# A decoder layer on one core: decay, query-key and value products restricted to the lower triangle

## The chip, the core and the metric

The kernel runs on one core of one Trainium2 chip. The core has TensorE (matmuls, results in eight banks of 512 f32 columns in PSUM), VectorE (DVE), ScalarE (ACT), GpSimd (POOL) and SyncE (SP), which only issues DMAs. Each engine works through its own queue in order; semaphores tie them together. The metric is the device time of one execution in microseconds (us), the median of several runs.

## What is computed

One decoder layer on 128 sequences of 128 tokens and 256 features: self-attention with one head, then a cross stage with eight heads of 32 features, gated and causal (queries and keys have the same length), then an FFN with a low-rank adapter. The change touches the cross stage alone. Its reference, cut:

```python
mask = jnp.tril(jnp.ones((seq, seq), dtype=bool))
F_act = jnp.where(mask, Fmat, -jnp.inf)          # Fmat[i, j] = csum[i] - csum[j]
Dtilde = F_act + itilde[..., None, :]
D = jnp.exp(Dtilde - max_d)
Ctilde = jnp.einsum('bhid,bhjd->bhij', qh, kh) * D / TAU
maxit = jnp.maximum(jnp.abs(jnp.sum(Ctilde, axis=-1, keepdims=True)), jnp.exp(-max_d))
Htilde = jnp.einsum('bhij,bhjd->bhid', Ctilde, vh) / (maxit + 1e-06)
```

D is zero wherever key j comes after query i, so of the 128x128 products per sequence and head only the lower triangle counts.

## The kernel before

The 128 sequences are taken in 32 groups of four (G = 4, a sequence of the group is called a batch b). The work is a software pipeline: in step `it` group it+1 is normalised (coming), group it is in self-attention (own), group it-1 is in the cross stage (cross) and group it-2 in the FFN (ffn). Steps 2 to 30 are one loop body, the rest is unrolled; steps 2 to 31 hold own, cross and ffn together. The order on every engine is the order in which its part of `step` is written out by hand; semaphores with a count per step (`c_ok`, `dexp_ok`, `pv_mm` and so on) connect the engines.

The cross stage on TensorE, for keys on the partitions and queries on the columns:

- `qk(t)` (L1255), t = 0 and 1, two batches each: for each batch 8 f32 matmuls, one per head. Head 4f+r has its 32 features on partitions 32r to 32r+31 of `ctxT` (stationary, 32x128) and `xn2T` (moving, 128 columns), so the four r work on four row tiles of the array and write four banks (QKB = TA, QQ, GT, DD). It stands among the eight FFN blocks `up(i)` (L1231, L1244), which use the full array. `keep_qk` (L653) on ScalarE copies the banks into `QKs`, four copies of 512 columns per call.
- `decay(b, hf)` (L1323): the logarithm of D for four heads, 512 columns, in DD or QQ: one bf16 matmul of `parts` with `moving`, and one that adds `later`, a mask of -1e30 above the diagonal. Eight such chunks per step. `dexp` (L674) on ScalarE takes the exponential into `dx` (the memory of `qT`), `weigh_qk` (L963) on VectorE multiplies it with `QKs` into `C`.
- `pv(b)` (L1338): 8 f32 matmuls, one per head, stationary the 32 value columns of `vc` (128x32), moving the 128 columns of `C`; head h writes partitions 32(h%4) on. Then `hs`, `turn_h`, `ht` and `head_sums` normalise.

The calls of L1387 to L1451 interleave these with `down` (L1302), `low_rank`, `adapt` (L1320), `turn_probs`, `mix` (L1375), `values` (L1382) of the other groups. `pv(b)` waits for the last chunk of C of its batch; `decay` waits until the chunk before last has been read by ScalarE.

`vc` is made by GpSimd (L555) early in the step; SyncE (L457 to L482) waits for it before it loads the next `ctxn`, then waits for `parts`.

## Time and profile before

| | us |
|---|---|
| median of 3 runs (1965.82 to 1968.34) | 1966.54 |
| the profiled execution | 1969.64 |
| its span, first to last instruction | 1967.8 |
| TensorE busy | 1905.0 (97%) |
| VectorE busy | 1509.3 (77%) |
| ScalarE busy | 1092.4 (56%) |
| GpSimd busy | 316.1 (16%) |

The profile splits TensorE into PE (matmuls) and PEld (loads of the stationary operand), which overlap. "L1269" is a line of the kernel. A row of a group gives the line, the engine, the operation, output<-inputs and the shapes; a row of the timeline begins with the start and the length in us, and merges neighbours of the same kind (x16), so that the last one's start is the first start plus the length less one's own duration. An f32 matmul appears as two records.

### The profile page before, as it was taken

The numbers are of one execution on the slowest core, as the hardware profiler recorded it, in microseconds if no ns is written. First come the engines' busy times: TensorE is split into PE (matmuls) and PEld (weight loads), VectorE is DVE, ScalarE is ACT, GpSimd is POOL, SyncE is SP. The second block draws the span as 40 slices with busy tenths as digits, with TensorE's granted clock in tenths as the row PEclk, the third lists the DMA queues.
The fourth block names the chain that finished last, engine by engine and source line by source line (L and its number), as shares of the span: only waits on it lengthen the run. The fifth ranks groups of instructions, "written<-read, shape, count | busy, mean of one in ns | idle before, by whom it ended". The sixth has DMA issues, their size and how long they took to land.

```text
span 1967.8 us, 44983 instructions
## 1 busy us (share of the span) xinstructions
PE 1905.0 (97%) x14612; PEld 1397.4 (71%) x14612; DVE 1509.3 (77%) x4352; ACT 1092.4 (56%) x2440; POOL 316.1 (16%) x259
## 2 busy tenths in 40 slices
PE   4689999999999999999999999999999999999988
PEld 3457777777777777777777777777777777777766
DVE  6588877778787778787778878777878777887742
ACT  2355556655556655556655555665555665555551
POOL 1111011111111111101111101111110111110110
PEclk9699999999999999999999999999999999999999
DMA  4101111111111111111111111111111111111100
GB/s 116 33 24 36 31 33 44 44 33 44 22 33 44 44 41 36 26 40 33 44 44 33 43 23 33 44 44 36 41 22 33 44 44 44 33 35 31 24 13 23
DMA packets 200751, 73.21 MB, mean 37 GB/s; under 512 B 148353, under 2 KB 200194, under 8 KB 200722
## 3 DMA queue, kind: packets, MB, share of 16 engines
q1 hardware_dynamic: 200722, 72.84, 14.5%
q8 instruction: 16, 0.26, 0.1%
q14 instruction: 13, 0.11, 0.0%
HBM read 53.93 MB, written 16.78 MB: 36 GB/s over the span
## 4 chain that ended last, share of the span: by engine, by line
PE 94%; DVE 4%; ACT 1%; issue 0%; DMA 0%; SPq 0%; DVEq 0%; ACTq 0%
PE UA L1302 16%; PE UB L1302 5%; PE UB L1244 5%; PE UA L1244 5%; PE TB L1244 5%; PE PV L1244 5%; PE UA L1252 3%; PE TA L1269 3%; PE TB L1382 3%; PE GT L1312 3%; PE TA L1382 3%; PE TA L1209 3%; PE TA L1113 3%; PE TB L1113 3%; PE UA L1320 2%; PE QQ L1332 2%
## 5 line engine op out<-in xcount | busy, mean ns | idle before, releaser
L1302 PE MATMUL UA<-W2f,hs_all 128*128 128x256 f32 x1536 | 349.0, 380 | 3.8 <-DVE ot L952 3.1
L1302 PEld LDWEIGHTS UA<-W2f,hs_all 128*128 128x128 f32 x1536 | 286.5, 190 | 63.1 <-issue 13.9
L968 DVE TENSOR_TENSOR C<-qT,QKs 128x512 f32<-128x512 f32 x256 | 166.6, 690 | 175.6 <-ACT qT L677 167.9
L562 POOL TENSOR_TENSOR Ng<-HT,gnw_b 128x256 f32<-128x256 f32 x128 | 96.1, 751 | 885.2 <-ACT HT L690 885.2
L543 POOL TENSOR_TENSOR xg<-x,gnb_b 128x1024 f32<-128x1024 f32 x32 | 76.4, 2386 | 679.5 <-ACT ot L632 646.0
L1302 PE MATMUL UB<-W2f,hs_all 128*128 128x256 f32 x512 | 115.8, 379 | 0.0
L576 ACT ACTIVATE lv<-ve 128x4 f32<-128x4 f32 x95 | 19.0, 200 | 161.2 <-DVE ve L795 161.2
L1302 PEld LDWEIGHTS UB<-W2f,hs_all 128*128 128x128 f32 x512 | 95.0, 190 | 11.7
L658 ACT ACTIVATE QKs<-TA 128x512 f32<-128x512 f32 x64 | 38.3, 599 | 105.6 <-PE DD L1269 105.6
L668 ACT ACTIVATE hs_all<-UA,b1c 128x512 f32<-128x512 f32 x64 | 44.0, 687 | 80.4 <-PE TB L1252 80.4
L1269 PEld LDWEIGHTS TA<-xn2T,ctxT 32*128 32x128 f32 x512 | 63.2, 190 | 26.2 <-issue 23.7
L549 POOL TENSOR_TENSOR x<-xin,cvp 128x1024 f32<-128x1024 f32 x32 | 76.4, 2387 | 26.7 <-DVE c L841 14.0
L902 DVE TENSOR_TENSOR_SCAN csum<-ones,lsig 128x128 f32<-128x128 f32 x32 | 79.6, 2489 | 1.1
L677 ACT ACTIVATE qT<-QQ 128x512 f32<-128x512 f32 x128 | 75.7, 591 | 6.3 <-PE QQ L1334 0.5
L1269 PE MATMUL TA<-xn2T,ctxT 32*128 32x128 f32 x512 | 75.6, 287 | 2.9 <-ACT QKs L658 2.2
L677 ACT ACTIVATE qT<-DD 128x512 f32<-128x512 f32 x128 | 75.1, 586 | 3.0 <-PE DD L1334 3.0
L1269 PE MATMUL QQ<-xn2T,ctxT 32*128 32x128 f32 x512 | 75.6, 288 | 0.0
L1269 PE MATMUL GT<-xn2T,ctxT 32*128 32x128 f32 x512 | 75.6, 288 | 0.0
L1269 PE MATMUL DD<-xn2T,ctxT 32*128 32x128 f32 x512 | 75.6, 288 | 0.0
L1252 PE MATMUL UA<-T,E 32*128 32x512 f32 x128 | 71.7, 640 | 0.0
L1252 PE MATMUL TB<-T,E 32*128 32x512 f32 x128 | 71.7, 640 | 0.0
L1252 PE MATMUL PV<-T,E 32*128 32x512 f32 x128 | 71.7, 640 | 0.0
(310 smaller groups left out, 5378.6 us busy)
## 6 DMA issues: line engine op xcount, KB each, us to landing
xin<-x SPq DMA_DIRECT2D x32, 512.0 KB, 3.5
ctxn<-ctx SPq DMA_DIRECT2D x32, 512.0 KB, 3.8
bands<-ctx SPq DMA_DIRECT2D x256, 64.0 KB, 2.0
out<-ot SPq DMA_DIRECT2D x32, 512.0 KB, 3.0
Ev<-xn SPq DMA_DIRECT2D x512, 1.0 KB
hs_all<-L_ffn_W SPq DMA_DIRECT2D x4, 512.0 KB, 8.9
T<-tok SPq DMA_DIRECT2D x128, 2.0 KB
moving<-parts SPq DMA_DIRECT2D x96, 8.0 KB, 1.8
```

The source lines that it names most:

```text
L543: pool.tensor_tensor(xg[:, :, :], x2[:, :, :], gnb_b[:, :].unsqueeze(1).broadcast_to([P, G, D]), ALU.add).then_inc(xg_ok.h, 1)
L549: pool.tensor_tensor(x2[:, :, :], xin[:, :, :], cvp[:, :].unsqueeze(1).broadcast_to([P, G, D]), ALU.add).then_inc(xb_ok.h, 1)
L562: pool.tensor_tensor(Ng[:, b, :].rearrange("p (k n) -> p k n", k=2), HT[:, b % 2, :, 0:P], gnw_b[:, :].rearrange("p (k n) -> p k n", k=2), ...
L677: act.activation(dx[hf], DB[hf][:, :], ACT.Exp)\
L902: dve.tensor_tensor_scan(csum[:, :], ones[:, :], lsig[:, :], 0.0, ALU.mult, ALU.add)\
L968: dve.tensor_tensor(C[:, b % 2, 4 * hf:4 * hf + 4, :].rearrange("p h i -> p (h i)"), dx[hf], QKs[:, b, 4 * hf:4 * hf + 4, :].rearrange("p ...
L1113: ins = pe.matmul(TAB[m][:, :], A_w[:, k, m * P:(m + 1) * P], xn1T[:, k, :], start=(k == 0), stop=(k == 1))
L1244: pe.matmul(UP[i % 4][:, :], w[:, k, hc * P:(hc + 1) * P], xt[:, k, :], start=(w is W1h and xt is xn3h and k == 0), stop=False)
L1252: pe.matmul(UP[r][:, :], E[32 * r:32 * r + 32, j, :], T[32 * r:32 * r + 32, :], start=False, stop=True).then_inc(up_mm.h, 1)
L1269: ins = pe.matmul(QKB[r][:, (2 * b + f) * P:(2 * b + f + 1) * P], ctxT[lane, f, tok], xn2T[lane, f, tok], start=True, stop=True)
L1302: ins = pe.matmul(OB[b][:, 0:D], hs_all[:, k, b * S:(b + 1) * S], W2f[:, k, :], start=(i == 0), stop=(i == KH - 1))
L1382: ins = pe.matmul(TAB[b // 2][:, (b % 2) * D:(b % 2) * D + D], pxT[:, k, b * S:(b + 1) * S], Wvp[:, k, :], start=(k == 0), stop=(k == 1))
```

## The change

With H = 64, the queries of a batch are split into late ones (64 to 127), which need all 128 keys, and early ones (0 to 63), which need only keys 0 to 63. The quarter early query, late key is no longer computed.

- Query-key: for each batch 8 matmuls with the same 128-column stationaries and the 64 late columns, then 8 with stationaries of 64 columns (the early keys) and the 64 early columns. Heads 0 to 3 (f = 0) go to partitions 0 to 63, heads 4 to 7 to partitions 64 to 127, so that two head groups share one block of 64 columns. A bank now holds 384 columns instead of 512.
- Decay: six chunks per step instead of eight. Three belong to a pair of batches: chunk 0 and chunk 2 are the late columns of the first and the second batch, 8 heads by 64; chunk 1 holds the early columns of both, packed on the upper and lower partitions by two matmuls of 64 stationary columns. `dexp` and `weigh_qk` run six times.
- Value product: for each batch 8 matmuls of 64 late columns from `vc`, and 8 of 64 early columns from `vcs`. `vcs` holds the early keys' values of heads 0 to 3 on partitions 0 to 63 and of heads 4 to 7 on partitions 64 to 127; its other halves stay zero. Two DMAs per step fill it from `vc`.
- `keep_qk` copies 384 columns. Two setup buffers move from `QKs` to `C`, setup gets one copy more (the mask for the lower partitions) and one memset (`vcs`).

The diff, cut to its core:

```diff
+H = S // 2
+CHUNKS = 3 * G // 2
...
-        QKs = sb("QKs", [P, G, HEADS, P])
+        QKs = sb("QKs", [P, G, 3 * CB, H])
+        vcs = sb("vcs", [P, G, 2, P])
...
-        C = sb("C", [P, 2, HEADS, P])
+        C = sb("C", [P, 4, HEADS, H])
...
+        vcs_loaded = per_step("vcs_loaded", CROSS, 2 * 16)
...
+                if CROSS.on(it):
+                    sp.wait_ge(vc_ok.h, vc_ok.at(it, 1))
+                    for f in range(2):
+                        sp.dma_start(vcs[H * f:H * f + H, :, f, :], vc[0:H, :, P * f:P * f + P])\
+                          .then_inc(vcs_loaded.h, 16)
...
-                        act.activation(QKs[:, 2 * t:2 * t + 2, r::4, :],
-                                       QKB[r][:, :].rearrange("p (b f i) -> p b f i", b=2, f=2), ACT.Copy)\
+                        act.activation(QKs[:, 2 * t:2 * t + 2, r::CB, :],
+                                       QKB[r][:, 0:6 * H].rearrange("p (b f i) -> p b f i", b=2, f=3), ACT.Copy)\
...
-                def dexp(b, hf):
-                    act.wait_ge(d_mm.h, d_mm.at(it, 2 * b + hf + 1))
-                    act.wait_ge(c_ok.h, c_ok.at(it, max(2 * b + hf - 1, 0)))
-                    act.activation(dx[hf], DB[hf][:, :], ACT.Exp)\
+                def dexp(k):
+                    act.wait_ge(d_mm.h, d_mm.at(it, k + 1))
+                    act.wait_ge(c_ok.h, c_ok.at(it, max(k - 1, 0)))
+                    act.activation(dx[k % 2], DB[k % 2][:, :], ACT.Exp)\
...
+            done(dve.tensor_copy(later[H:P, 0:H], later[0:H, 0:H]))
...
-                def weigh_qk(b, hf):
-                    k = 2 * b + hf
+                def weigh_qk(k):
+                    t, j = k // 3, k % 3
                     dve.wait_ge(dexp_ok.h, dexp_ok.at(it, k + 1))
-                    dve.wait_ge(QKs_ok.h, QKs_ok.at(it, 4 * (b // 2) + 4))
+                    dve.wait_ge(QKs_ok.h, QKs_ok.at(it, 4 * t + 4))
+                    if j == 1:
+                        dve.tensor_tensor(C[:, 2 + t, :, :].rearrange("p (b r) i -> p b (r i)", b=2),
+                                          dx[k % 2].rearrange("p (b x) -> p b x", b=2),
+                                          QKs[:, 2 * t:2 * t + 2, HEADS:HEADS + CB, :].rearrange("p b r i -> p b (r i)"),
+                                          ALU.mult).then_inc(c_ok.h, 1)
+                        return
+                    b = 2 * t + j // 2
                     dve.wait_ge(pv_mm.h, pv_mm.at(it, max(b - 1, 0)))
-                    dve.tensor_tensor(C[:, b % 2, 4 * hf:4 * hf + 4, :].rearrange("p h i -> p (h i)"), dx[hf],
-                                      QKs[:, b, 4 * hf:4 * hf + 4, :].rearrange("p h i -> p (h i)"), ALU.mult)\
+                    dve.tensor_tensor(C[:, b % 2, :, :].rearrange("p h i -> p (h i)"), dx[k % 2],
+                                      QKs[:, b, 0:HEADS, :].rearrange("p h i -> p (h i)"), ALU.mult)\
                         .then_inc(c_ok.h, 1)
...
+                        early, late = slice(tok.start, tok.start + H), slice(tok.start + H, tok.stop)
                         for f in range(2):
                             for r in range(4):
                                 lane = slice(32 * r, 32 * r + 32)
-                                ins = pe.matmul(QKB[r][:, (2 * b + f) * P:(2 * b + f + 1) * P],
-                                                ctxT[lane, f, tok], xn2T[lane, f, tok], start=True, stop=True)
+                                pe.matmul(QKB[r][:, (3 * b + f) * H:(3 * b + f + 1) * H],
+                                          ctxT[lane, f, tok], xn2T[lane, f, late], start=True, stop=True)
+                        for f in range(2):
+                            for r in range(4):
+                                lane = slice(32 * r, 32 * r + 32)
+                                ins = pe.matmul(QKB[r][H * f:H * f + H, (3 * b + 2) * H:(3 * b + 3) * H],
+                                                ctxT[lane, f, early], xn2T[lane, f, early], start=True, stop=True)
...
-                def decay(b, hf):
-
-                    k = 2 * b + hf
+                def decay(k):
+
+                    t, j = k // 3, k % 3
                     pe.wait_ge(dexp_ok.h, dexp_ok.at(it, max(k - 1, 0)))
                     if k == 0:
                         pe.wait_ge(QKs_ok.h, QKs_ok.at(it, 8))
                         pe.wait_ge(parts_ok.h, parts_ok.at(it, 1))
                         pe.wait_ge(moving_loaded.h, moving_loaded.at(it, 3 * 16))
-                    h0 = HEADS * b + 4 * hf
-                    pe.matmul(DB[hf][:, :], parts[:, 0, :], moving[:, h0:h0 + 4, :],
-                              start=True, stop=True)
-                    ins = pe.matmul(DB[hf][:, :], ident_h[:, :], later[:, :].unsqueeze(1).broadcast_to([P, 4, P]),
+                    bank = DB[k % 2]
+                    if j == 1:
+                        heads = moving[:, 2 * t * HEADS:(2 * t + 2) * HEADS, 0:H].rearrange(
+                            "p (b f r) i -> p f b r i", b=2, f=2)
+                        for f in range(2):
+                            pe.matmul(bank[H * f:H * f + H, :], parts[:, 0, 0:H], heads[:, f, :, :, :],
+                                      start=True, stop=True)
+                    else:
+                        b = 2 * t + j // 2
+                        pe.matmul(bank[:, :], parts[:, 0, :], moving[:, HEADS * b:HEADS * b + HEADS, H:P],
+                                  start=True, stop=True)
+                    mask = later[:, 0:H] if j == 1 else later[:, H:P]
+                    ins = pe.matmul(bank[:, :], ident_h[:, :], mask.unsqueeze(1).broadcast_to([P, HEADS, H]),
                                     start=False, stop=True, skip_group_check=True)
...
-                    pe.wait_ge(c_ok.h, c_ok.at(it, 2 * b + 2))
+                    pe.wait_ge(c_ok.h, c_ok.at(it, 3 * (b // 2) + 2 + b % 2))
                     if b == 0:
                         pe.wait_ge(vc_ok.h, vc_ok.at(it, 1))
+                        pe.wait_ge(vcs_loaded.h, vcs_loaded.at(it, 2 * 16))
                     elif b == 1:
                         pe.wait_ge(h_ok.h, h_ok.at(it, 6))
                     bank = PB[b % 2]
                     for h in range(HEADS):
                         q = 32 * (h % 4)
-                        ins = pe.matmul(bank[q:q + 32, (h // 4) * P:(h // 4 + 1) * P], vc[:, b, HD * h:HD * h + HD],
-                                        C[:, b % 2, h, :], start=True, stop=True)
+                        pe.matmul(bank[q:q + 32, (h // 4) * P + H:(h // 4 + 1) * P], vc[:, b, HD * h:HD * h + HD],
+                                  C[:, b % 2, h, :], start=True, stop=True)
+                    for f in range(2):
+                        for r in range(4):
+                            ins = pe.matmul(bank[HD * r:HD * r + HD, f * P:f * P + H], vcs[:, b, f, HD * r:HD * r + HD],
+                                            C[:, 2 + b // 2, 4 * (b % 2) + r, :], start=True, stop=True)
...
-                    decay(0, 0)
-                    decay(0, 1)
+                    decay(0)
+                    decay(1)
                 if ffn:
                     down(0)
                     low_rank()
                 if cross:
-                    decay(1, 0)
+                    decay(2)
                     pv(0)
-                    decay(1, 1)
+                    decay(3)
                     turn_em()
                 if own:
                     turn_probs()
                 if cross:
                     turn_h(0)
-                    decay(2, 0)
                 if ffn:
                     adapt(0)
                 if cross:
                     pv(1)
-                    decay(2, 1)
+                    decay(4)
                 if own:
                     mix(0)
                 if cross:
@@ -1412,9 +1445,8 @@
                 if own:
                     mix(1)
                 if cross:
-                    decay(3, 0)
                     pv(2)
-                    decay(3, 1)
+                    decay(5)
```

What stands on TensorE for one query-key call, before: the end of `up(4)`, then four groups like the one shown (the shape is stationary columns x moving columns), then `up(5)`.

```order
L1244 MATMUL UA<-xn3l,W1h 128x512 x2
L1257 REGISTER_ALU
L1269 MATMUL TA<-xn2T,ctxT 128x128
L1269 MATMUL QQ<-xn2T,ctxT 128x128
L1269 MATMUL GT<-xn2T,ctxT 128x128
L1269 MATMUL DD<-xn2T,ctxT 128x128
...
L1239 REGISTER_ALU
L1244 MATMUL UB<-xn3h,W1h 128x512 x2
```

And after, where the two kinds take turns batch by batch:

```order
L1258 MATMUL UA<-xn3l,W1h 128x512 x2
L1271 REGISTER_ALU
L1284 MATMUL TA<-xn2T,ctxT 128x64
L1284 MATMUL QQ<-xn2T,ctxT 128x64
L1284 MATMUL GT<-xn2T,ctxT 128x64
L1284 MATMUL DD<-xn2T,ctxT 128x64
...
L1289 MATMUL TA<-xn2T,ctxT 64x64
L1289 MATMUL QQ<-xn2T,ctxT 64x64
L1289 MATMUL GT<-xn2T,ctxT 64x64
L1289 MATMUL DD<-xn2T,ctxT 64x64
...
L1258 MATMUL UB<-xn3h,W1h 128x512 x2
```

Each of the four banks now gets 8 matmuls per call where it got 4, in four blocks of two shapes.

Around the value product of batch 1, on TensorE, before:

```order
L1356 MATMUL PV<-centre,HS 128x132 x2
L1326 REGISTER_ALU
L1332 MATMUL DD<-moving,parts 128x512
L1334 MATMUL DD<-later,ident_h 128x512
L1319 ISA
L1320 MATMUL UA<-Ev,gT 128x256
L1349 MATMUL UB<-C,vc 32x128 x8
L1332 MATMUL QQ<-moving,parts 128x512
L1334 MATMUL QQ<-later,ident_h 128x512
```

And after:

```order
L1390 MATMUL PV<-centre,HS 128x132 x2
L1339 ISA
L1340 MATMUL UA<-Ev,gT 128x256
L1370 REGISTER_ALU
L1379 MATMUL UB<-C,vc 32x64 x8
L1383 MATMUL UB<-C,vcs 32x64 x8
L1356 MATMUL DD<-moving,parts 64x512 x2
L1363 MATMUL DD<-later,ident_h 128x512
L1409 MATMUL TA<-PT,xn 128x128 x4
```

The chunk between `turn_h(0)` and `adapt(0)` is gone, the value product has two halves, and the chunk behind it is an early one (chunk 4).

## Rows read from the trace of the kernel before

**Rows 1.** The page: busy time by engine, and the chain that ended last.

```profile
PE 1905.0 (97%) x14612; PEld 1397.4 (71%) x14612; DVE 1509.3 (77%) x4352; ACT 1092.4 (56%) x2440; POOL 316.1 (16%) x259
...
PE 94%; DVE 4%; ACT 1%; issue 0%; DMA 0%; SPq 0%; DVEq 0%; ACTq 0%
```

**Rows 2.** Busy time in two full steps, by window; columns as in the header.

```profile
core 0: us, PE busy (x) PEld busy (x) DVE busy (x) ACT busy (x) POOL busy (x), PEclk, DMA share, GB/s
998.60:1056.90 58.30, 58.30 (x453) 42.82 (x452) 46.66 (x136) 33.92 (x77) 9.70 (x7) 1.00 0.15 37
1056.90:1115.20 58.30, 58.30 (x453) 42.83 (x452) 46.64 (x136) 33.92 (x77) 9.70 (x7) 1.00 0.15 37
```

**Rows 3.** Timeline of PE around one query-key call: start us, length us, instruction.

```profile
1011.85 0.63 PE L1244 MATMUL UA<-xn3l,W1h 128*128 128x512 f32 x2
1012.40 0.37 PE L1269 MATMUL TA<-xn2T,ctxT 32*128 32x128 f32 x1
...
1012.42 0.37 PE L1269 MATMUL DD<-xn2T,ctxT 32*128 32x128 f32 x1
1012.62 0.27 PE L1269 MATMUL TA<-xn2T,ctxT 32*128 32x128 f32 x1
...
1012.73 0.27 PE L1269 MATMUL TA<-xn2T,ctxT 32*128 32x128 f32 x1
...
1013.31 0.27 PE L1269 MATMUL DD<-xn2T,ctxT 32*128 32x128 f32 x1
1013.51 0.50 PE L1244 MATMUL UB<-xn3h,W1h 128*128 128x512 f32 x1
```

**Rows 4.** Timeline of setup: products with one moving column.

```profile
24.66 0.53 PEld L1151 LDWEIGHTS QQ<-bcol,QKs 128*128 128x128 f32 x4
24.68 0.58 PE L1151 MATMUL QQ<-bcol,QKs 128*128 128x1 f32 x4
```

**Rows 5.** Timeline of PE around two value products and two decay chunks.

```profile
1026.84 0.38 PE L1334 MATMUL DD<-later,ident_h 128*128 128x512 bf16 x1
...
1027.15 0.38 PEld L1349 LDWEIGHTS PV<-C,vc 128*32 128x32 f32 x16 [0.43 <-issue]
1027.15 0.65 PE L1349 MATMUL PV<-C,vc 128*32 128x128 f32 x16
...
1027.73 0.39 PE L1332 MATMUL QQ<-moving,parts 99*128 99x512 bf16 x1
...
1029.17 0.38 PE L1332 MATMUL DD<-moving,parts 99*128 99x512 bf16 x1
...
1029.39 0.38 PE L1334 MATMUL DD<-later,ident_h 128*128 128x512 bf16 x1
...
1029.61 0.59 PE L1320 MATMUL UA<-Ev,gT 128*128 128x256 f32 x2
...
1031.16 1.05 PE L1375 MATMUL TA<-PT,xn 128*128 128x128 f32 x8
...
1033.39 0.38 PE L1332 MATMUL DD<-moving,parts 99*128 99x512 bf16 x1
```

**Rows 6.** Timeline of setup: pairs of 64-column tiles.

```profile
37.06 1.16 PE L1168 MATMUL GT<-ident,hs_all 128*64 128x128 f32 x16
```

**Rows 7.** Groups by line and form: count, then busy us and mean ns.

```profile
L677 ACT ACTIVATE qT<-QQ 128x512 f32<-128x512 f32 x128 | 75.7, 591 | 6.3 <-PE QQ L1334 0.5
L658 ACT ACTIVATE QKs<-TA 128x512 f32<-128x512 f32 x64 | 38.3, 599 | 105.6 <-PE DD L1269 105.6
L683 ACT ACTIVATE HS<-UB 128x256 f32<-128x256 f32 x64 | 24.7, 385 | 20.3 <-PE UB L1349 20.1
L968 DVE TENSOR_TENSOR C<-qT,QKs 128x512 f32<-128x512 f32 x256 | 166.6, 690 | 175.6 <-ACT qT L677 167.9
```

**Rows 8.** Timelines of POOL and of SP's queue early in the same step.

```profile
1008.91 1.96 POOL L555 TENSOR_TENSOR vc<-ctxn 128x992 f32<-128x992 f32 x1
...
1011.04 0.38 SPq L465 DMA_DIRECT2D ctxn<-ctx  x1
1014.57 0.56 SPq L469 DMA_DIRECT2D moving<-parts  x1
```

**Rows 9.** The cross step without an FFN, by window; columns as in rows 2.

```profile
79.00:99.00 20.00, 12.54 (x113) 7.94 (x117) 13.68 (x42) 11.17 (x33) 0.10 (x1) 0.53 0.27 54
```

More of the change, by code:

```diff
@@ L284, in build @@
         wT = stage[:, 1536:3072].rearrange("p (w k d) -> p w k d", w=3, k=KD)
-        wp = stage[:, 3072:3584].rearrange("p (k o) -> p k o", k=KD)
-        bB = stage[:, 3584:4096].rearrange("p (w k n) -> p w k n", w=2, k=KD)
+        spare = C[:, :, :, :].rearrange("p a b c -> p (a b c)")
+        wp = spare[:, 0:512].rearrange("p (k o) -> p k o", k=KD)
+        bB = spare[:, 512:1024].rearrange("p (w k n) -> p w k n", w=2, k=KD)
         bcol = sb("bcol", [P, 6])
@@ L328, in build @@
         em_mm = per_step("em_mm", CROSS, 1)
-        d_mm = per_step("d_mm", CROSS, 2 * G)
+        d_mm = per_step("d_mm", CROSS, CHUNKS)
         qk_mm = per_step("qk_mm", CROSS, 2)
@@ L350, in build @@
         em_ok = per_step("em_ok", CROSS, 1)
[L351 removed]
+        dexp_ok = per_step("dexp_ok", CROSS, CHUNKS)
         HS_ok = per_step("HS_ok", CROSS, G)
@@ L373, in build @@
         zo_ok = per_step("zo_ok", FFN, 1)
-        c_ok = per_step("c_ok", CROSS, 2 * G)
+        c_ok = per_step("c_ok", CROSS, CHUNKS)
         x2_ok = per_step("x2_ok", SELF, G)
@@ L530, in _ @@
                                pattern=[[-8, G], [-32, CB], [-1, R]], channel_multiplier=1)
-            for t in (WgT, Z, Zo, E, T, Ev, em):
+            for t in (WgT, Z, Zo, E, T, Ev, em, vcs):
                 pool.memset(t[tuple([slice(None)] * len(t.shape))], 0.0)
@@ L714, in step @@
                         .then_inc(em_ok.h, 1)
-                    dexp(0, 0)
-                    dexp(0, 1)
+                    dexp(0)
+                    dexp(1)
                 if coming:
@@ L721, in step @@
                 if cross:
-                    dexp(1, 0)
+                    dexp(2)
                     hs(0)
-                    dexp(1, 1)
+                    dexp(3)
                     ht(0)
@@ L728, in step @@
                 if cross:
-                    dexp(2, 0)
                     hs(1)
-                    dexp(2, 1)
+                    dexp(4)
                 if own:
@@ L744, in step @@
                 if cross:
-                    dexp(3, 0)
                     hs(2)
-                    dexp(3, 1)
+                    dexp(5)
                     ht(2)
@@ L1001, in step @@
                 if cross:
-                    weigh_qk(0, 0)
-                    weigh_qk(0, 1)
+                    weigh_qk(0)
+                    weigh_qk(1)
                 if ffn:
@@ L1009, in step @@
                 if cross:
-                    weigh_qk(1, 0)
-                    weigh_qk(1, 1)
+                    weigh_qk(2)
+                    weigh_qk(3)
                     dve.wait_ge(em_mm.h, em_mm.at(it, 1))
@@ L1014, in step @@
                     head_sums(0)
-                    weigh_qk(2, 0)
-                    weigh_qk(2, 1)
+                    weigh_qk(4)
                 if ffn:
@@ L1028, in step @@
                 if cross:
-                    weigh_qk(3, 0)
-                    weigh_qk(3, 1)
+                    weigh_qk(5)
                 if coming:
@@ L1459 @@
 V_BIAS = V_WT + 2 + 2 + 2 + 4
-SETUP_V = V_BIAS + 2 + 1 + 2 + 1 + 8 + 1
+SETUP_V = V_BIAS + 2 + 1 + 1 + 2 + 1 + 8 + 1
 def kernel(**inputs):
```

3 lines of the change are left out of this document (1 added, 2 removed).

## The prediction, made before the changed kernel was run

> **What bounds the kernel now.** I read the page first: TensorE is busy 97% of the span and carries 94% of the chain that ended last [rows 1]. Then two neighbouring steps of the loop, by window: each takes 58.30 us, TensorE is busy for all of it at the full granted clock, VectorE for 46.7 and ScalarE for 33.9 [rows 2]. There are 30 such full steps (the four batches of a group in their cross stage while another group is in its self stage and a third in its FFN), 1,749 of 1,967.8 us; the rest is setup, one cross step without an FFN at the start, and the drain at the end. So a full step costs what TensorE's stream costs, and everything the change saves on the other two engines is hidden. The question is how TensorE's stream changes, and the timeline of its instructions gives the prices. The profiled execution took 1969.64 us, span 1967.8; I make the sum as a difference and put it on the median of the three runs, 1966.54, from which the profile is 3.1 us off.
>
> **How a small product is priced.** An f32 product is two records for each of its matmuls. In the query-key call four 32-row tiles run side by side: the four first records start within 0.02 us, and then a new group of four starts every 0.11 us (1012.62, 1012.73, ... 1013.29) [rows 3]. 0.11 us is what 128 moving columns cost, but it is also what the stationary operand costs: in setup, four records of a product with 1 moving column and the same 128 stationary columns take 0.58 us, 0.25 of it the last one's own latency, so 0.11 each [rows 4]. Halving the moving columns of a product whose stationary is still 128 columns wide therefore saves nothing. The second price is that of a change of the array's shape. Between two full-array matmuls of 512 bf16 columns the starts are 0.22 apart; from the last full one to the first 32-column one it is 0.31 (1026.84 to 1027.15), and back from the last 32-column record (its start is 1027.15 + 0.65 - 0.27 = 1027.53) to the full array 0.20 where 0.11 would be its own width [rows 5]. The query-key call shows the same: 1012.08 (1011.85 + 0.63 - 0.40) to 1012.40 is 0.32 against a pitch of 0.23, and 1013.31 to 1013.51 is 0.20 [rows 3]. Each change costs about 0.09 us, and behind it the first load is not covered: 0.10 for 128 f32 columns (the second group starts 0.22 after the first, not 0.11), so by width 0.05 for 64 and 0.03 for 32.
>
> **Query-key (L1263 to L1271), per call, two calls per step.** Before: 8 groups, 1.10 us from 1012.40 to 1013.51 [rows 3]. After: per batch 4 groups with 128-column stationaries and 64 moving columns, then 8 matmuls on 32x64 tiles, and so twice. The late part keeps its 4 groups of 0.11 per batch; only the last of each ends 0.05 earlier: -0.11. The early part is new: if the upper and the lower column tiles run together it is 2 groups of 0.06 (64 columns, twice) per batch: +0.22. Three more changes of shape (late to early, back, late to early) at 0.09: +0.28; the uncovered first loads behind them, 0.05 + 0.10 + 0.05: +0.21; and 0.02 of staggered starts for each of three more bursts: +0.06. Sum +0.67 per call, **+1.33 per step**. Bounds: no row shows a change from a 32x128 to a 32x64 tile. If it is free, only the early groups are added, +0.22 per call, +0.44 per step; if the two column tiles take turns, +0.22 more per call, +1.8 per step. I take the middle, since every change of shape in rows 3 and 5 costs 0.09, and since 64-column tiles do run in pairs in setup: 16 records in 1.16 us, 0.06 apart, where 128 f32 columns one after the other would need 0.11 each [rows 6].
> The Trainium skill (TensorEngine Tiling (Array Packing), Key Properties) says that changing the tiling mode drains TensorE, while tiles of one mode work independently, and lists 32x128 and 32x64 as different configurations. By that rule the term is +1.33; if only the rows of the array counted it would be +0.44. The trace agrees on the changes that it has (0.09 us each).
>
> **Decay (L1323 to L1336), per step.** Before: 8 chunks of two matmuls at 0.22 [rows 5], 3.52. After: four late chunks as before, and two early ones: two 64-column matmuls side by side (0.22), the mask (0.22), and changes of shape. The first early chunk stands between full-array work: two changes and one uncovered load, 0.24, so 0.68. The second comes right behind pv(1), where a change is due anyway: 0.58. Sum 1.76 + 1.26 = 3.02: **-0.50 per step**. Bounds: -0.88 if the changes are free, -0.07 if the two 64-column matmuls take turns; again rows 6 are nearest to side by side.
>
> **Value product (L1338 to L1351), per batch, four per step.** Before: 16 records in groups of four, 0.58 us from 1027.15 to 1027.73 [rows 5]. After: 32 records of 64 columns, all on 128x32 tiles, so no change of shape in between: 8 groups of 0.055 to 0.06 in the place of 4 of 0.11, the same columns. The 16 loads of 32 columns take 0.38 from first start to last end at 0.11 latency each [rows 5], so they overlap and hide behind 0.055. **+0.03 per batch, +0.1 per step**; bounds 0 and, if a group cannot start sooner than 0.11 after the last, +0.38 per batch, +1.5 per step.
>
> **What is hidden.** ScalarE loses two exponentials (0.59 each) and a fifth of eight copies of 512 columns (0.60 against 0.39 at 256, so about 0.49 at 384); VectorE loses two products of 0.65 to 0.69 [rows 7]. None of it is on the path of a full step. Cover: there is now no decay between mix(1) and pv(2). pv(2) needs chunk 4, whose mask ends about 0.4 us after its start, then 0.59 of ScalarE, 0.69 of VectorE and some 0.2 of handing over; TensorE has mix(0), turn_h(1) and mix(1) in between, 1031.16 to 1033.39 [rows 5], 2.2 us, so some 0.5 remains. If it failed, pv(2) would wait that long. The same holds for chunk 5 and pv(3). The two DMAs that fill vcs stand on SyncE's queue behind vc (ready at 1010.87) and ahead of the ctxn load; each issue is 0.4 to 0.6 us, and the queue is idle from 1011.42 to 1014.57 [rows 8]; pv(0) wants them at 1027, so nothing. Setup gets one more small copy and a memset, ahead of work that waits elsewhere: nothing.
>
> **The two partial steps.** In the cross step without an FFN the granted clock is 0.53 [rows 9], the lower of two levels (1.2 GHz), so TensorE's extra work costs double there, about 2 us; against it stand waits on ScalarE and VectorE that shrink by about as much. At the end the same waits shrink by 1 or 2 us. I count nothing, -3 to +2.
>
> **Sum.** 1.33 - 0.50 + 0.10 = +0.93 per step, times 30 = +28 us: 1966.5 + 28 = **1994 us**. The change cuts columns only where the stationary operand and the shape of the array do not matter, in a quarter of the decay.
>
> **Rivals.**
> (a) Free changes of shape, faster than before. Place: the three new boundaries in each query-key call and those around the early decay chunks. If these cost nothing and the value product costs nothing, the step changes by 0.44 - 0.88 = -0.44, -13 us, 1953. It decides as soon as all three new boundaries and loads of a call cost less than 0.2 us together instead of 0.55. For it: no row shows such a boundary between two shapes with the same 32 rows. Against: all other boundaries show 0.09. 12%.
> (b) No change to be measured: either the loads of four 32-row tiles are quicker than the 0.11 of rows 4 (the late groups then shrink to 0.06, -0.45 per call, and the step's sum is +0.03), or the query-key boundaries alone are free (+0.44 - 0.50 + 0.10 = +0.04). About 1968. 12%.
> (c) The early tiles take turns, or handing over costs a bit more at 64 columns: +0.45 per step, 1994 + 13 = 2007. 11%.
> (d) Starts are the limit. A change that doubles the records pays if a record cannot follow the last in less than 0.027 us (16 records in 0.37 us of starts is 0.025 on average in rows 5, and rows 3 give 0.028). Then the value product costs +1.5 and the early query-key groups +1.3 more per step, 2.8 x 30 = 84 us: 2075. Against it: within a group the starts are under 0.01 apart. 8%.
> The Trainium skill (TensorE: Matmul & The Clock Gate, "Wait — 56ns, not 53.3ns?") states that start-to-start never falls below about 25 ns however small a matmul is; taken for every tile it would give rival (d), but its section on packing small matmuls gives 4 ns between tiles, and the starts in rows 3 are that close.
>
> **How the numbers follow.** Forecast as summed, 1980 to 2005 by the small uncertainties of its terms: 57%. Taking (a) to (d): slower 57 + 11 + 8 = 76%, same 12%, faster 12%. The range leaves out (d) and most of (a): 1960 to 2030. About 0.2%, 4 us, is what a measurement of this kernel can tell from no change.
>
> **What would show it.** In the profile after, a full step of about 59.2 us with TensorE still busy throughout. A query-key call of 1.75 to 1.8 us to the next FFN matmul, with groups of the late part 0.11 apart, of the early part 0.06, and gaps of about 0.15 at the three boundaries. A value product of 0.6 us with 32 records; early decay chunks of 0.6 to 0.7. ScalarE and VectorE at 32 and 45 us per step. The prediction is wrong if late groups start 0.06 apart, if there is no gap between late and early, if the value product takes 0.9, or if TensorE begins to wait for C ahead of pv(2) or pv(3).

## The result, and the profile after

The changed kernel takes 1993.39 us in the median of four runs (1990.73 to 1998.63), the kernel before 1967.05 in the same comparison (four runs, 1965.82 to 1968.34): ratio 1.0137, 95% interval 1.0115 to 1.0159, so 26 us slower. The prediction was 1994 us.

The page of the changed kernel, busy time by engine, and one line of its costliest groups (the ScalarE copy of the scores):

```profile
PE 1934.3 (97%) x18644; PEld 1437.5 (72%) x18644; DVE 1469.1 (74%) x4289; ACT 1042.5 (52%) x2376; POOL 318.0 (16%) x260
...
L668 ACT ACTIVATE QKs<-TA 128x384 f32<-128x384 f32 x64 | 31.6, 493 | 165.3 <-PE DD L1289 165.3
```

Against [rows 1] TensorE is busy 29 us more, VectorE 40 and ScalarE 50 us less. What was saved, was saved on the other engines; the chain that ended last is TensorE's for 94%, as before. A full step by window (columns as in rows 2; the next step reads the same):

```profile
1013.92:1073.09 59.17, 59.17 (x579) 44.01 (x578) 45.44 (x134) 32.37 (x75) 9.73 (x7) 1.00 0.16 41
```

A full step is 59.17 us for 58.30 [rows 2], and TensorE is still busy for all of it. 0.87 x 30 = 26.1 us, of the 26.3 by which the medians differ; in the medians the partial steps add nothing. (The profiled execution, at 1998.63, is 5 us over its median. There is one trace of this kernel, which does not show what part of it took longer than usual; the run without the value DMAs below has the same step and took 1992.65, and 4.3 us of the 6.0 between the two stand ahead of the second full step.) The step repeats to 0.02 us from one to the next, so in what follows the length of a full step is the measure, and the time of a run is given beside it.

**The query-key call.** Timeline of TensorE around the first half of a call in the changed kernel. L1284 is the late product, L1289 the early one; of each group of four simultaneous tiles one record stands here:

```profile
1027.73 0.32 PE L1284 MATMUL TA<-xn2T,ctxT 32*128 32x64 f32 x1
...
1027.89 0.27 PE L1284 MATMUL TA<-xn2T,ctxT 32*128 32x64 f32 x1
...
1028.00 0.27 PE L1284 MATMUL TA<-xn2T,ctxT 32*128 32x64 f32 x1
...
1028.13 0.27 PE L1284 MATMUL DD<-xn2T,ctxT 32*128 32x64 f32 x1
1028.33 0.27 PE L1289 MATMUL TA<-xn2T,ctxT 32*64 32x64 f32 x1
...
1028.48 0.22 PE L1289 MATMUL DD<-xn2T,ctxT 32*64 32x64 f32 x1
1028.63 0.32 PE L1284 MATMUL TA<-xn2T,ctxT 32*128 32x64 f32 x1
...
1029.39 0.22 PE L1289 MATMUL DD<-xn2T,ctxT 32*64 32x64 f32 x1
1029.53 0.74 PE L1258 MATMUL UB<-xn3h,W1h 128*128 128x512 f32 x2
```

The late groups start 0.11 apart with 64 columns as they did with 128 [rows 3]. From the last late record to the first early one it is 0.20 (1028.13 to 1028.33); the sixteen early records start within 0.15; from the last of them to the next late one, or to the FFN's product, 0.15 (1028.48 to 1028.63, 1029.39 to 1029.53). One batch takes 0.90 us, the call 1.80 (1027.73 to 1029.53) where it was 1.10: +0.70 per call, +1.40 per step.

**Values and decay.** Timeline of TensorE around the first early chunk, and from the value product of batch 0 to the early chunk ahead of the mixing products (L1363 mask, L1379 late and L1383 early values, L1360 late and L1356 early decay):

```profile
1037.25 0.38 PE L1363 MATMUL DD<-later,ident_h 128*128 128x512 bf16 x1
1037.56 0.41 PE L1356 MATMUL QQ<-moving,parts 99*64 99x512 bf16 x2
...
1038.12 3.62 PE L1322 MATMUL UA<-W2f,hs_all 128*128 128x256 f32 x16
...
1044.07 0.43 PE L1379 MATMUL PV<-C,vc 128*32 128x64 f32 x16
1044.31 0.41 PE L1383 MATMUL PV<-C,vcs 128*32 128x64 f32 x16
1044.65 0.39 PE L1360 MATMUL QQ<-moving,parts 99*128 99x512 bf16 x1
1044.88 0.38 PE L1363 MATMUL QQ<-later,ident_h 128*128 128x512 bf16 x1
1045.10 0.27 PE L1398 MATMUL GT<-ident,em 128*128 128x128 f32 x1
1045.21 0.60 PE L1403 MATMUL TB<-ident,y 128*128 128x128 f32 x4
1045.64 0.62 PE L1390 MATMUL PV<-centre,HS 128*128 128x132 f32 x4
1046.10 0.59 PE L1340 MATMUL UA<-Ev,gT 128*128 128x256 f32 x2
1046.62 0.43 PE L1379 MATMUL UB<-C,vc 128*32 128x64 f32 x16
...
1047.20 0.41 PE L1356 MATMUL DD<-moving,parts 99*64 99x512 bf16 x2
1047.54 0.39 PE L1363 MATMUL DD<-later,ident_h 128*128 128x512 bf16 x1
```

A value product is 0.58 us (1044.07 to 1044.65), as before, with twice the records. An early chunk behind a value product is 0.34 for the pair of 64-column matmuls (1047.20 to 1047.54) and 0.23 for the mask, 0.57; a late chunk is 0.45 (1044.65 to 1045.10). The first early chunk stands between full-array work: from the mask of the late chunk before it to the FFN product behind it 0.87 us pass (1037.25 to 1038.12), 0.22 of them that mask's own, so 0.65 to 0.66.

### The profile page after: what moved, and what is told of

The parts are those of the page before. It is cut to its first block, busy times and chain, and to the rows that moved or that the text cites. A ratio compares the mean times of both kernels' runs of the same rounds, so it can differ in the third digit from the quotient of the medians.

```text
span 1996.6 us, 52832 instructions
## 1 busy us (share of the span) xinstructions
PE 1934.3 (97%) x18644; PEld 1437.5 (72%) x18644; DVE 1469.1 (74%) x4289; ACT 1042.5 (52%) x2376; POOL 318.0 (16%) x260
## 4 chain that ended last, share of the span: by engine, by line
PE 94%; DVE 4%; ACT 1%; issue 0%; DMA 0%; SPq 0%; DVEq 0%; ACTq 0%
PE UA L1322 16%; PE UB L1322 5%; PE UB L1258 5%; PE UA L1258 5%; PE TB L1258 5%; PE PV L1258 5%; PE TA L1284 3%; PE UA L1266 3%; PE TB L1416 3%; PE GT L1332 3%; PE TA L1416 3%; PE TA L1223 3%; PE TA L1127 3%; PE TB L1127 3%; PE UA L1340 2%; PE QQ L1115 2%
## 5 line engine op out<-in xcount | busy, mean ns | idle before, releaser
L984 DVE TENSOR_TENSOR C<-qT,QKs 128x512 f32<-128x512 f32 x128 | 88.6, 692 | 219.4 <-ACT qT L687 206.3
L668 ACT ACTIVATE QKs<-TA 128x384 f32<-128x384 f32 x64 | 31.6, 493 | 165.3 <-PE DD L1289 165.3
L1284 PEld LDWEIGHTS TA<-xn2T,ctxT 32*128 32x128 f32 x512 | 67.7, 189 | 30.3 <-issue 23.9
L1284 PE MATMUL TA<-xn2T,ctxT 32*128 32x64 f32 x512 | 85.4, 287 | 2.5 <-ACT QKs L668 1.8
L1284 PE MATMUL QQ<-xn2T,ctxT 32*128 32x64 f32 x512 | 85.5, 287 | 0.0
L1284 PE MATMUL GT<-xn2T,ctxT 32*128 32x64 f32 x512 | 85.5, 287 | 0.0
L1284 PE MATMUL DD<-xn2T,ctxT 32*128 32x64 f32 x512 | 85.5, 287 | 0.0
L1266 PE MATMUL UB<-T,E 32*128 32x512 f32 x128 | 71.7, 640 | 0.0
L1416 PE MATMUL TA<-Wvp,pxT 128*128 128x256 f32 x256 | 67.3, 387 | 0.7 <-ACT pxT L714 0.7
```

Source lines behind the costliest of these rows:

```text
L984: dve.tensor_tensor(C[:, b % 2, :, :].rearrange("p h i -> p (h i)"), dx[k % 2], QKs[:, b, 0:HEADS, :].rearrange("p h i -> p (h i)"), ALU.m ...
L1266: pe.matmul(UP[r][:, :], E[32 * r:32 * r + 32, j, :], T[32 * r:32 * r + 32, :], start=False, stop=True).then_inc(up_mm.h, 1)
L1284: pe.matmul(QKB[r][:, (3 * b + f) * H:(3 * b + f + 1) * H], ctxT[lane, f, tok], xn2T[lane, f, late], start=True, stop=True)
L1416: ins = pe.matmul(TAB[b // 2][:, (b % 2) * D:(b % 2) * D + D], pxT[:, k, b * S:(b + 1) * S], Wvp[:, k, :], start=(k == 0), stop=(k == 1))
```

## The experiments

The theory: the step is TensorE's own stream, and in it the stationary operand and the changes of the array's shape cost, not the moving columns. Rivals: the number of products and loads costs (then order doesn't matter); the columns do cost (then halving them helped); the engines that were relieved, or the new DMAs, play a part.

### One change of shape in a call instead of three (late_first)

```diff
-for b in range(2): late(b); early(b)
+for b in range(2): late(b)
+for b in range(2): early(b)
```

> Of the changed kernel, each query-key call runs the late products of both batches first and then the early products of both, so that a call changes the matmul's shape once inside instead of three times; nothing is left out. If the price of the early products is the change of shape (the trace of the changed kernel shows 0.20 us before the first early product and 0.15 us before the next late one), two of these stretches go, and a call falls from 1.806 to about 1.49 us, a full step by 0.63 us and the kernel by 19 us, to about 1974 us. If the price is the number of products and of weight loads, the call stays at 1.8 us and the kernel at 1993 us.

Measured: 1976.28 us (six runs) against 1968.29 for the kernel before, ratio 1.0039, interval 1.0027 to 1.0052. The step, and the timeline of a call at its start, at the boundary and at its end:

```profile
1002.65:1061.14 58.49, 58.49 (x579) 43.61 (x578) 45.46 (x134) 32.32 (x75) 9.72 (x7) 1.00 0.17 41
```

```profile
1016.45 0.32 PE L1283 MATMUL TA<-xn2T,ctxT 32*128 32x64 f32 x1
...
1017.29 0.27 PE L1283 MATMUL DD<-xn2T,ctxT 32*128 32x64 f32 x1
1017.50 0.27 PE L1290 MATMUL TA<-xn2T,ctxT 32*64 32x64 f32 x1
...
1017.76 0.22 PE L1290 MATMUL DD<-xn2T,ctxT 32*64 32x64 f32 x1
1017.91 0.50 PE L1258 MATMUL UB<-xn3h,W1h 128*128 128x512 f32 x1
```

The same 32 matmuls (64 records) in another order take 1.46 us a call (1016.45 to 1017.91), 0.34 less, and the step is 0.68 shorter. The price is the change of shape: the rival that counts products and loads had said no difference. The two changes that went were worth 0.17 us each.

### No early products at all (no_early_qk)

```diff
-for f in range(2):
-    for r in range(4): pe.matmul(QKB[r][H*f:H*f+H, ...], ctxT[lane, f, early], xn2T[lane, f, early])
```

> Of the changed kernel, the early query-key products are left out, so the early queries' scores are not computed. All that the early products cost should go: both boundaries and the 0.15 us that the 16 of them take, twice a call. A call falls from 1.806 to about 1.10 us, the value that it had in the kernel before with whole products, a full step by 1.4 us and the kernel by 42 us, to about 1951 us. If the saving were only that of their columns (32 products side by side in 0.3 us a call), the step would fall by 0.6 us and the kernel by 18 us.

Measured: 1949.14 us in one run, full step:

```profile
987.96:1045.61 57.65, 57.65 (x516) 42.91 (x515) 45.46 (x134) 32.31 (x75) 9.72 (x7) 1.00 0.16 42
```

The step is 1.52 shorter than that of the changed kernel, 0.76 a call. By the trace of this run, a call of late products alone, all eight groups with half the columns, takes 1.05 us, against 1.10 for the whole products of before. So a call that computes half of the scores is as long as one that computes them all, to 0.05 us, and everything that is added for the early quarter is loss.

### The late products with 128 columns again (wide_late)

```diff
-pe.matmul(QKB[r][:, 64 columns],  ctxT[lane, f, tok], xn2T[lane, f, late])
+pe.matmul(QKB[r][:, 128 columns], ctxT[lane, f, tok], xn2T[lane, f, tok])
```

The heads of f = 1 run ahead of those of f = 0 here, each block of 128 columns lies so that only its unused half is overwritten, and `keep_qk` copies the columns where the wanted scores now lie.

> Of the changed kernel, the late query-key products run with 128 moving columns again instead of 64 (the 64 further columns hold nothing that is used; the early products overwrite or nobody reads them). If a pair of late products is held by its two 128-row weight loads, as I read the pitch of 0.11 us, halving the columns bought nothing and this costs between 0 and 0.05 us per call, 0 to 3 us of the kernel (1993 to 1996 us). If the halved columns did buy time (0.055 us per two products, eight pairs a call), a call is 0.45 us longer and the kernel 27 us longer, about 2020 us.

Measured: 2001.01 us (four runs), ratio 1.0171, interval 1.0155 to 1.0188. Step and one batch's late groups:

```profile
1010.98:1070.36 59.38, 59.38 (x579) 44.02 (x578) 45.43 (x134) 32.28 (x75) 9.71 (x7) 1.00 0.16 41
```

```profile
1024.78 0.37 PE L1284 MATMUL TA<-xn2T,ctxT 32*128 32x128 f32 x1
...
1024.99 0.27 PE L1284 MATMUL TA<-xn2T,ctxT 32*128 32x128 f32 x1
...
1025.11 0.27 PE L1284 MATMUL TA<-xn2T,ctxT 32*128 32x128 f32 x1
```

The groups are 0.11 apart with either number of columns, so the stationary sets their pace. But the step is 0.21 longer, 0.11 per call: twice what the expectation allowed. The place is the first group of each batch: the second starts 0.21 after it (1024.78 to 1024.99) and not 0.16 (1027.73 to 1027.89), so behind a change of shape the time of the group's own columns adds to that of the next load. That is the -0.11 per call of the prediction's own sum, at the front of a batch and not at its end as it had put it.

### One full-width matmul for an early decay chunk (decay_full, pt_first)

```diff
-for f in range(2): pe.matmul(bank[H*f:H*f+H, :], parts[:, 0, 0:H], heads[:, f])
+pe.matmul(bank[:, :], parts[:, 0, :], heads[:, 0])          # and later[H:P, 0:H] = -1e30
```

The stationary holds all 128 keys, and the mask blots out the late 64.

> Of the changed kernel, the early decay chunks use one product of the full width (heads 0 to 3) in place of the two packed 64-row ones, so heads 4 to 7 have no early decay. If the two packed products run side by side and the saving is theirs less the change of shape, a chunk of one full-width 128-column product without a change of shape takes about 0.44 us, as a late chunk does, instead of 0.656 and 0.565: 0.33 us less per full step, 10 us less for the kernel, about 1983 us. If the two packed products took turns, the saving would be larger than 0.2 us per chunk, 0.5 us or more per step.

Measured: 1996.16 us in one run. (This one execution was 1.8 us behind the profiled one of the changed kernel, at 1998.63, when its second full step began, 187.3 for 185.5 us; by the step it is shorter.) Step:

```profile
1013.32:1072.32 59.00, 59.00 (x578) 43.92 (x576) 45.44 (x134) 32.18 (x75) 9.71 (x7) 1.00 0.16 41
```

Only 0.17 less and not 0.33. The chunks themselves are about as expected, 0.44 and 0.46. The loss is behind the second one. ScalarE and TensorE there:

```profile
1046.25 0.58 ACT L718 ACTIVATE PT<-TB 128x512 f32<-128x512 f32 x1
...
1046.64 0.38 PE L1362 MATMUL DD<-later,ident_h 128*128 128x512 bf16 x1
...
1046.88 0.52 PEld L1408 LDWEIGHTS TA<-PT,xn 128*128 128x128 f32 x4 [0.36 <-ACT PT L718]
1046.88 0.60 PE L1408 MATMUL TA<-PT,xn 128*128 128x128 f32 x3
```

The mixing product needs ScalarE's copy of the turned probabilities, which ends at 1046.83. Its first load and the product itself start together at 1046.88, so the load is no longer ahead of the product: a wait that neither kernel had. In the changed kernel (ScalarE and loads, then TensorE) and, below it, the turning of the probabilities in the kernel before:

```profile
1047.04 0.58 ACT L718 ACTIVATE PT<-TB 128x512 f32<-128x512 f32 x1
...
1047.67 0.63 PEld L1409 LDWEIGHTS TA<-PT,xn 128*128 128x128 f32 x5
1047.77 0.62 PE L1409 MATMUL TA<-PT,xn 128*128 128x128 f32 x4
```

```profile
1028.29 0.60 PE L1369 MATMUL TB<-ident,y 128*128 128x128 f32 x4
```

Here the load still starts 0.10 ahead of the product, but no more than 0.05 behind the end of the copy (1047.62): no cover is left. In the kernel before, the probabilities were turned 2.87 us ahead of the mixing (1028.29 to 1031.16 [rows 5]), since a decay chunk stood between them; now it is 2.56 (1045.21 to 1047.77). The change took 0.3 us of cover away, just up to the point where the wait begins. To see that it is this wait, the next run gives ScalarE another order.

```diff
 dexp(3)
+PT_copy()
 ht(0)
-PT_copy()
```

> The run with the full-width early decay (heads 4 to 7 have no early decay) with one more edit: ScalarE copies the turned probabilities before it copies and squares the head sums of batch 0. If the 0.094 us by which TensorE's first mixing products came late there is the wait for that copy, the copy is now ready 1 us earlier, this wait goes and the full step falls from 59.00 to about 58.91 us. If the wait is for something else (a weight load, or a bank), the step stays at 59.00; if the later copy of the head sums becomes the last to arrive somewhere, it is longer than 59.00.

Measured: 1987.90 us in one run, step 58.87 for 59.00:

```profile
1006.78:1065.65 58.87, 58.87 (x577) 44.01 (x576) 45.47 (x134) 32.31 (x75) 9.72 (x7) 1.00 0.16 41
```

```profile
1038.52 0.60 ACT L718 ACTIVATE PT<-TB 128x512 f32<-128x512 f32 x1
...
1040.11 1.08 PEld L1409 LDWEIGHTS TA<-PT,xn 128*128 128x128 f32 x8
```

The copy is now ready 1 us before its load, and the step gains 0.13: the wait was for it. The place is right too: from the mask behind the second early chunk to the end of the eight mixing products it is 1.24 us in the run before this one (1046.64 to 1047.88) and 1.10 here (1040.11 to 1041.21), 0.13 by the unrounded starts. With it 0.30 of the expected 0.33 is there. The rest, and a bit more, went into the sixteen FFN products behind the first early chunk: from the first start to the last they take 3.28 us, as in the kernel before, where the changed kernel has 3.24. TensorE is busy for all of the step in both runs, so that figure does not show such a wait.

### Is ScalarE's idle time free? (act_extra)

```diff
 dexp(k)
+if k in (2, 4): act.activation(idle_out, 512 columns, Copy)
```

> The changed kernel with one more ScalarE copy of 512 columns (about 0.6 us) behind the exponential of chunk 2 and of chunk 4; nothing is left out. ScalarE is busy 32 of 59 us, so if only busy shares count this costs nothing (59.17 us a step, 1993 us). By the run with the full-width early decay, TensorE's first mixing product waits for ScalarE's copy of the turned probabilities as soon as it would start 0.01 to 0.05 us earlier; the first extra copy fills 0.40 us of idle time ahead of the head sums' copy and delays that copy by about 0.2 us, and with it the turned probabilities: +0.2 us per full step at the least, +6 us for the kernel, and more if the second copy delays something too.

Measured: 1998.60 us in one run (the profiled execution of the changed kernel had 1998.63), step:

```profile
1011.31:1070.57 59.26, 59.26 (x580) 44.06 (x578) 45.48 (x134) 32.94 (x77) 9.62 (x7) 1.00 0.16 41
```

```profile
1042.05 0.62 ACT L691 ACTIVATE idle_out<-A_w 128x512 f32<-128x512 f32 x1
...
1042.57 0.38 ACT L696 ACTIVATE HS<-PV 128x256 f32<-128x256 f32 x1
...
1043.00 0.52 PEld L1393 LDWEIGHTS PV<-centre,HS 128*128 128x128 f32 x4
1043.03 0.69 PE L1393 MATMUL PV<-centre,HS 128*128 128x132 f32 x4
...
1043.55 0.59 PE L1343 MATMUL UA<-Ev,gT 128*128 128x256 f32 x2
```

+0.09 and neither +0.2 nor 0. ScalarE is idle for 45% of the step, and a copy put into that time still costs. It costs at another place than I had said, though: it pushes back the copy of the value sums (HS, ends at 1042.95), so that the first load of their turning products starts 0.03 ahead of its product instead of 0.10 (1045.54 and 1045.64 in the changed kernel), and the four take 0.52 us to the next product (1043.03 to 1043.55) instead of 0.46 (1045.64 to 1046.10). The copy of the probabilities comes later with it, but so does TensorE, and no second wait is added. From the turning of the probabilities to the mixing it is 2.64 us (1042.59 to 1045.23) for 2.56, 0.08 of the 0.09, so the second extra copy, which comes later, cost nothing.

### No DMAs for the early values (no_vcs_dma)

```diff
-for f in range(2): sp.dma_start(vcs[H*f:H*f+H, :, f, :], vc[0:H, :, P*f:P*f+P])
```

> The changed kernel without the two DMAs that move the early values to the other partitions, so the early half of the value products is zero. I put these DMAs at nothing, since they land some 20 us before their products run: 59.17 us a step, 1993 us, unchanged within 0.1%. If they or SP's time for issuing them delayed a load, the step would be shorter.

Measured: 1992.65 us in one run, and a full step of 59.17 us by window, as with them. In a full step the DMAs are free.

### Whole query-key products, packed decay (swapped, halves, halves_pt)

The runs say which half of the change pays: the decay (-0.54 a step), not the scores (+1.40). The packing of the early decay needs the early keys of heads 4 to 7 on the upper partitions. The change got them there by small query-key products on another column tile. If instead the two halves of the keys stand in swapped order for heads 4 to 7 from the load on, a whole 128x128 product puts them there for nothing.

```diff
-sp.dma_start(ctxn[:, :, :], c_g[it])
+sp.dma_start(ctxn[:, :, 0:P], c_g[it][:, :, 0:P])
+for u in range(2):       # heads 4 to 7: late keys first
+    sp.dma_start(ctxn[H*u:H*u+H, :, P:D], c_g[it][H-H*u:P-H*u, :, P:D])
...
-late and early products of qk(t)
+pe.matmul(QKB[r][:, 128 columns], ctxT[lane, f, tok], xn2T[lane, f, tok])
...
-pe.matmul(bank[:, :], parts[:, 0, :], moving[:, 8 heads, H:P])
+for f in range(2):       # keys = early | late | early
+    pe.matmul(bank[:, 256*f:256*f+256], keys[:, H*f:H*f+P], moving[:, 4 heads of f, H:P])
```

With it come a mask for each order of the halves, a transposition of `ctxT` in three pieces, two multiplications of 64 partitions each for an early chunk on VectorE, and two copies there that build `keys`. The two DMAs that fill `vcs` stay.

> A kernel that keeps only the packed decay and the packed values of the change: the query-key products are whole again (8 of 128x128 per batch, no change of shape inside a call), and for heads 4 to 7 the late keys stand on partitions 0 to 63 and the early ones on 64 to 127, so that the early halves of both head groups already lie on different partitions and need no packed products. Nothing is left out. By my sum the query-key term goes (call back to 1.10 us), the decay term stays (-0.54 us per full step against the kernel before), the values cost +0.04: a full step of 57.8 us, -0.5 us against before, 15 us for the kernel, about 1952 us. If ScalarE or VectorE set the end of a stage once TensorE is quicker (as the run with a full-width early decay showed, where 0.10 of 0.27 us came back as a wait for a copy), or the three transposes and the second product of a late chunk cost as much as the decay saves, it is at 1968 us, no different from before.

Measured: 1956.47 us (five runs), ratio 0.9946, interval 0.9933 to 0.9960; step 57.80. In this run both products that fill a bank for a late chunk have `start=True`, and the kernel does not compute the reference. The next run differs in this one flag (`start=(f == 0)`: the mask is then added to both halves) and computes all of the reference.

> The kernel with whole query-key products and the swapped key halves of heads 4 to 7, with one line mended: of the two products that fill a bank for a late decay chunk only the first clears the bank's marks for accumulation, so that the mask is added to both halves of the bank. Nothing is left out. The same instructions as in the run before it, so the same time: 1956 us, 0.5% under the kernel before, full step 57.8 us. If the marks had cost time, it would differ from 57.8 us.

Measured: 1956.56 us (six runs) against 1966.51, ratio 0.9946, interval 0.9934 to 0.9958: 0.5% less than the kernel before, little but clear of the noise, and, at 57.80 us a step, 1.37 us a step shorter than the change.

```profile
990.90:1048.70 57.80, 57.80 (x520) 43.32 (x519) 46.58 (x140) 33.15 (x75) 9.74 (x7) 1.00 0.17 42
```

The step was forecast to 0.01 us: -0.50. The whole time was not: 30 x 0.50 = 15 us, and 10 came. In the two profiled executions it is 13.2 us (spans of 1954.6 and 1967.8); 3 of the missing 5 are that the profiled execution of the kernel before is 3.1 us above its median, and no trace shows where executions of one kernel differ. The rest is at the end, where TensorE waits for others. From the scores of the last full step on (1800.20 here, 1814.80 before) it took 154.4 us for 153.0, though one of the 30 full steps lies there, 0.5 us shorter: 1.9 us are lost. The granted clock falls below its full level in a stretch where the kernel before kept it. The last cross stage, this kernel and then the kernel before (whose next window reads 1.00 too):

```profile
1884.60:1894.60 10.00, 7.93 (x136) 4.39 (x135) 7.92 (x16) 5.11 (x12) 1.64 (x2) 0.96 0.00 1
1894.60:1904.60 10.00, 8.88 (x67) 7.45 (x65) 5.13 (x15) 3.43 (x9) 1.46 (x2) 0.70 0.01 2
```

```profile
1897.80:1907.80 10.00, 10.00 (x83) 5.73 (x82) 5.07 (x11) 7.59 (x14) 0.76 (x1) 1.00 0.01 1
```

A mean of 0.70 over 10 us is 6 us at the lower level (1.2 GHz) of its two, and 4 at the upper (2.4 GHz). TensorE was busy 7.93 of 10 us in the window in which it fell; the changed kernel was busy 7.86 of 10 us in a window there (1936.6 to 1946.6) and kept its clock. The kernel before in turn has more of the lower level earlier: 0.75 and 0.91 in the windows from 1867.8 to 1887.8, for 0.83 and 1.00 here at the same distance from the end. Over the last 160 us, summed by windows, the lower level holds for 10.2 us here and for 6.8 before, and 3.4 us more at half the speed would cost up to 1.7 us, an estimate close to the 1.9 that are lost. That the clock is what costs them was not tried by itself.

The last run adds ScalarE's other order to it.

> The same kernel, and ScalarE copies the turned probabilities ahead of the head sums of batch 0. TensorE does not wait for that copy here (its early decay chunk is the packed one, and the mixing products behind it start without a wait, with 0.01 to 0.05 us to spare), so by my reading this gains nothing: 57.80 us a step and 1956 us, within 0.1%. If the copy is a bound even so, the step falls by up to 0.1 us, 3 us for the kernel; if the head sums' copy, now 0.2 us later, is waited for, the step is longer.

Measured: 1957.73 us (six runs), ratio 0.9950, interval 0.9937 to 0.9962, step 57.80: no gain, as expected. With the packed early chunk ahead of them the mixing products do not wait for the copy.

## Why the prediction was right, step by step

- **What bounds.** TensorE is busy for all of the step in every run, and what VectorE and ScalarE save (1.2 and 1.6 us a step) does not show in its length. Right, with one reserve: a step in which TensorE is busy throughout can hold a wait of 0.1 us for ScalarE all the same (decay_full, act_extra).
- **Query-key, predicted +1.33 a step, measured +1.40.** The groups of 0.11 that the stationary holds: shown by wide_late and by no_early_qk. Early products side by side: sixteen records within 0.15 us per batch, 0.31 a call where the sum had 0.22 + 0.06 (its rounded terms add up to 0.66 a call, not 0.67). The boundaries: the sum had 0.49 for changes and uncovered loads together; measured 0.20 + 0.15 + 0.20 at the three new ones and 0.15 for 0.20 at the exit, 0.50. The single gap into the early products was put at 0.15 and is 0.20. That number stood in rows 3 already, as the exit of the call (1013.31 to 1013.51): it is the late products that leave slowly, whoever follows. The prediction had taken 0.05 off there for the halved columns; they came off at the first group of a batch instead, so the total held. Rival (a), free changes, fell with late_first, as did the second form of (b), free changes in the call alone; the first form of (b), quicker loads, fell with the pitch of 0.11 in the changed kernel and in wide_late. Rival (c), early tiles in turn, fell with the 0.15 us for sixteen records.
- The Trainium skill (TensorEngine Tiling (Array Packing), Key Properties and Available Configurations) says that a change of tiling mode drains TensorE and counts 32x128 and 32x64 as two configurations. The runs agree: a change between these two costs what the others do, 0.20 us from 32x128 to 32x64 (1028.13 to 1028.33) as from 32x128 to the full array (1013.31 to 1013.51 [rows 3]).
- **Decay, predicted -0.50, measured -0.54.** Chunk 1 took 0.65 to 0.66 for 0.68, chunk 4 0.57 for 0.58. Right, side by side. The two chunks that went were 0.44 each.
- **Values, predicted +0.1, measured +0.04.** 0.585 against 0.577 a batch, by the unrounded starts. The 32 records start within 0.43 us (1044.07 to 1044.31 + 0.41 - 0.22), 0.014 apart on average, so rival (d), a floor of 0.027 a record, is out.
- **Hidden things.** The DMAs: nothing, by no_vcs_dma. The cover of pv(2) held, with more to spare than the 0.5 us of the prediction: VectorE has the weighted chunk 4 ready at 1049.29 (row below), and pv(2) starts at 1050.11, right behind mix(1). TensorE does not wait ahead of pv(3) either. What the prediction missed is the cover that the moved chunk had given to ScalarE's copy of the probabilities: it shrank from 0.3 us to about nothing. In the changed kernel this order was not tried by itself; in the kernel with whole query-key products, whose early chunk is the same, the copy 1 us earlier gains nothing (halves_pt). In the run with the quicker early chunk it took 0.13 of the 0.33 us (decay_full against pt_first).

```profile
1048.60 0.69 DVE L977 TENSOR_TENSOR C<-qT,QKs 128x512 f32<-128x512 f32 x1 [0.54 <-ACT qT L687]
```

- **Partial steps, counted at nothing:** 30 steps of +0.87 are 26.1 of the 26.3 us between the medians. That it is so exact is in part luck: the two profiled executions differ by 28.8 us in their spans, 2.7 of it outside the 0.87 per full step.

The sum was +0.93 a step and +0.87 came: +1.40 - 0.54 + 0.04 = +0.90, and 0.03 less elsewhere, mostly in the sixteen FFN products behind chunk 1 (3.24 us for 3.28 from the first start to the last). The three terms missed by +0.07, -0.04 and -0.06, so the forecast came within 1 us also because its errors cancel.

## What to carry to other kernels

Before cutting a product to its useful part, see what holds its pace: with an f32 stationary of 128 columns, cutting the moving columns from 128 to 64 gained nothing here, but for 0.05 us in the first group behind a change of shape. Count the boundaries between array shapes that the cut brings (0.15 to 0.20 us from start to start here) and put equal shapes together; better, move the data so that the whole product already leaves it where the packed part needs it. And when a chunk is taken out from between two others, ask whose operand its time was covering.

## What the runs showed that I had not expected

- The gap at a change of shape depends on the side that leaves: 0.20 us behind 32x128 products, whether the FFN's full array or a 32x64 tile follows, 0.15 behind 32x64 products (1028.13 to 1028.33, 1028.48 to 1028.63, 1029.39 to 1029.53). The value products do the same: 0.20 with 128 moving columns (1027.53 to 1027.73 [rows 5]), 0.15 with 64 (1044.50 to 1044.65). In all of these the gap is the pace of the groups that leave (0.11, or 0.055 to 0.06) and 0.09 us for the change. So the prediction's 0.09 was right, and the late products keep their pace of 0.11 up to the gap.
- Behind a change of shape the first group's moving columns do count: 0.05 us for 64 of them (wide_late against the changed kernel), where inside a run of groups they don't.
- ScalarE's copies of 256, 384 and 512 columns from PSUM take 385 and 599 ns [rows 7] and 493 ns (the page after).
